# An attention loop with its PSUM banks re-dealt: scores and turned scores as one block per step, turning back by single transposes, projections on other steps

## The chip, the cores and the metric

The kernel runs on one core of a Trainium2 chip. The metric is the device time of the run in microseconds (us). TensorE (PE in the profile) multiplies matrices and writes to PSUM, which has eight banks; VectorE (DVE), ScalarE (ACT) and GpSimd (POOL) do the rest, SyncE (SP) issues DMAs. Each engine works through its own instructions in order, and waits on semaphores for the others.

## The reference

The input is x, 32 sequences of 125 frames with 23 features. Five neighbouring frames form a patch, so a sequence has L = 121 tokens, and there are 3,872 tokens of D = 128 channels:

```python
y = relu(patches @ W.T + b)                       # 115 -> 128
h = (y - mean(y)) * rsqrt(var(y) + eps) * gamma + beta     # over all tokens
a = layernorm(h)
q, k, v = (a @ w.T + b for w, b in ...)           # 8 heads of 16
scores = q @ k.T / 4 + col_bias                   # per sequence and head, 121 x 121
h = h + (softmax(scores) @ v) @ o_w.T + o_b
z = layernorm(h)
e = argmax(z @ Wr + br)                           # one of 8 experts, gate 1
out = h + relu(z @ W1[e] + b1[e]) @ W2[e] + b2[e]
```

col_bias is one number per head and column, from the last valid edge that points at the column. All arithmetic is float32 here.

## The kernel before, in words

A prologue builds the patches, the batch norm's statistics and the weights. Then comes the **attention loop**: 38 steps `t` (`STEPS = B + 6`), one sequence per step, and later pieces of a sequence some steps behind its scores. Two sequences make a pair `p = t // 2`; what is done once for a pair sits in its even or its odd step. After the loop the experts' part goes through 38 tiles of 128 rows.

What a step holds, by the names in the trace (`psS`, `psO`, `psU`, `psB` are PSUM):

- PE `scores` (lines 921, 928): q·k of sequence t and the turned scores k·q of sequence t-1, eight matmuls each (two passes each in the trace), in waves of four that use the four 32-row groups of the array. They come in two halves ("parts") with other matmuls between.
- DVE `nmax` (line 750) takes the maximum of each score row, PE turns it (line 1044), DVE `qm` (line 765) adds it to q, so that the turned scores come out with the maximum subtracted. ACT `PT` (line 495) is exp of the turned scores, PE line 1052 multiplies by V, ACT `OTs` copies, PE line 1005 turns back, DVE `rden` and `on` (736, 738) divide, PE 1025 turns, ACT `oT` copies, PE 1001 multiplies by the output weights, DVE 744 adds to `rows`, DVE 759 squares for the second norm, POOL `rstd2` (365, 370) makes rs2, ACT 489 and DVE `lg` (723) use it.
- Once for a pair, ahead of its scores: ACT `batch_norm` (h0T, 434), PE `transpose_h0` (893), ACT `h0_copy` (h0k, 441), DVE `squares1` (635), POOL `norm1_first` and `norm1_second` (var 345, rs 349, xn 353 and 357, rows 359), PE `transpose_xn` (899), ACT `xT_copy` (448), PE `project` (904) for k and q, DVE `k_copy` (kT, 661), ACT `q_copy` (qT, 453), PE `values` (910), ACT `v_copy` (460).
- For a group of four or two sequences DVE picks experts (`expert_max` and the like), PE ranks rows (`rank_rows`, 967 to 972), DVE gives places (`row_places`), and POOL writes one sequence's rows per step to their places by an indirect DMA (`scatter_rows`, 376).

The order is written out by hand, engine by engine. Three facts of it matter. `h0k` is a single buffer: `h0_copy` of pair p+3 waits (semaphore s_h0b, line 440) until POOL has done `norm1_second` of pair p+2, its last reader. POOL's order in the even step t = 2p is `norm1_first(p + 2)`, one scatter, `rstd2`; in the odd step it is `norm1_second(p + 2)`, one scatter, `rstd2` (lines 388 to 396). And `norm1_first(p + 2)` waits for `squares1(p + 2)`, which DVE does in the even step.

## Time and profile before

| | |
|---|---|
| median of 3 runs | 311.4 us (311.34 to 316.01) |
| the profiled execution | 310.43 us, of which 308.7 us are the span from first to last instruction |
| attention loop at its steady pace | 58.5 to 199.0 us of the span |
| its end, and the experts' bookkeeping | 199.0 to 221.4 us |
| experts' tiles | 221.4 to 308.7 us |
| busy over the span | PE 85%, DVE 61%, ACT 54%, POOL 46% |

The profile's times are in us from the start of the span. A timeline row gives start, duration, engine, line, operation, output<-input, shapes, and in brackets how long the engine had been idle before it and who released it. Close instructions of one kind are merged to one row (x4). [...]

### The profile page before, as it was taken

What the parts mean: (1) busy time and instruction counts of PE and PEld (TensorE: products, weight loads), DVE (VectorE), ACT (ScalarE), POOL (GpSimd) and SP (SyncE); (2) the same over time, 40 slices, a digit from 0 to 9 for tenths busy, and PEclk for the clock granted to TensorE, in tenths of its full rate; (3) what the DMA queues carried; (4) which work ended last, traced back from release to release, by engine and by line L of the source; (5) the groups of instructions that cost most, each with busy time, mean ns of one, the idle gap of its engine ahead of it and who ended that gap; (6) DMA issues with size and microseconds to landing.
All of it is one profiled execution on the core that took longest, in us unless ns stands there. A gap on an engine that the chain in (4) does not pass through costs nothing.

```text
span 308.7 us, 9094 instructions
## 1 busy us (share of the span) xinstructions
PE 263.8 (85%) x2915; PEld 223.6 (72%) x2915; DVE 187.5 (61%) x690; ACT 165.3 (54%) x395; POOL 141.8 (46%) x256
## 2 busy tenths in 40 slices
PE   3898479999999999999999999883099999999960
PEld 2767357778778777877778786562099999999960
DVE  3887233476777768677686777746436556555540
ACT  3861122566655666466664654521067777777730
POOL 7000640343438646476565654347215555555560
PEclk9995575999999999999999999955579999999996
DMA  3200399100001101010010110111243334334200
GB/s 104 71 2 0 98 345 317 47 3 2 2 3 35 32 18 35 19 37 25 28 32 19 34 35 18 35 52 49 74 115 86 101 87 120 98 93 122 79 7 0
DMA packets 15374, 19.14 MB, mean 62 GB/s; under 512 B 4007, under 2 KB 11467, under 8 KB 15328
## 3 DMA queue, kind: packets, MB, share of 16 engines
q1 hardware_dynamic: 11888, 12.15, 14.0%
q0 software_dynamic: 3296, 6.00, 6.6%
q8 instruction: 25, 0.41, 0.6%
q10 hardware_dynamic: 144, 0.41, 0.4%
q14 instruction: 21, 0.17, 0.2%
HBM read 10.58 MB, written 8.47 MB: 62 GB/s over the span
## 4 chain that ended last, share of the span: by engine, by line
PE 71%; issue 9%; POOL 7%; DVE 5%; ACT 3%; DMA 2%; SPq 1%; POOLq 0%; DVEq 0%
PE psS L1089 11%; PE psS L921 10%; PE psB L904 9%; PE psO L1052 5%; PE psO L1100 5%; PE psU L1100 5%; PE psU L1001 4%; PE psU L1005 4%; PE psB L893 3%; POOL region_d L376 3%; PE psB L910 2%; DVE nmax L750 2%; ACT patT L421 2%; PE psU L1044 2%; PE psS L928 2%
## 5 line engine op out<-in xcount | busy, mean ns | idle before, releaser
L404 POOL DMA_INDIRECT out<-y_out,sidx x38 | 36.9, 971 | 45.6 <-DVE y_out L824 41.2
L495 ACT ACTIVATE PT<-psS 121x968 f32<-121x968 f32 x32 | 31.3, 977 | 37.7 <-PE psS L928 37.7
L921 PE MATMUL psS<-kT,qT 32*121 32x121 f32 x512 | 45.7, 294 | 4.9 <-ACT xT L448 2.0
L376 POOL DMA_INDIRECT region_d<-rows,pos x32 | 34.7, 1085 | 31.2 <-DVE pos L709 21.2
L928 PE MATMUL psS<-qm,kT 32*121 32x121 f32 x512 | 45.7, 295 | 0.0
L833 DVE TENSOR_SCALAR hT<-psS,b1T 128x128 f32<-128x128 f32 x76 | 23.3, 347 | 34.9 <-PE psS L1089 34.8
L921 PEld LDWEIGHTS psS<-kT,qT 32*121 32x121 f32 x512 | 34.1, 185 | 13.7 <-issue 9.3
L1089 PE MATMUL psS<-xgT,W_tile 128*128 128x128 f32 x304 | 41.7, 282 | 0.0
L750 DVE TENSOR_REDUCE nmax<-psS 121x8 f32<-121x968 f32 x32 | 37.0, 1157 | 5.6 <-PE psS L921 5.5
L1089 PEld LDWEIGHTS psS<-xgT,W_tile 128*128 128x128 f32 x304 | 38.5, 199 | 0.0
L928 PEld LDWEIGHTS psS<-qm,kT 32*121 32x121 f32 x512 | 33.6, 185 | 0.4 <-DVE qm L765 0.3
L536 ACT ACTIVATE hT<-psS,b1T 128x128 f32<-128x128 f32 x76 | 23.8, 363 | 13.6 <-PE psS L1089 13.3
L510 ACT ACTIVATE W_tile<-W_sb 128x512 f32 x38 | 23.9, 630 | 10.0 <-DVE eid L800 3.7
L765 DVE TENSOR_TENSOR qm<-qT,psU 128x242 f32<-128x242 f32 x32 | 13.0, 407 | 15.8 <-PE psU L1044 15.8
L365 POOL TENSOR_SCALAR var<-ss 121x1 f32<-121x1 f32 x32 | 6.3, 198 | 33.3 <-DVE sq L759 32.8
L736 DVE RECIPROCAL rden<-psU 121x8 f32<-121x8 f32 x32 | 6.7, 208 | 24.4 <-PE psU L1005 24.4
L1052 PE MATMUL psO<-PT,V 121*32 121x121 f32 x512 | 20.3, 276 | 0.4 <-ACT oT L498 0.4
L1100 PE MATMUL psU<-W_sb,hT 128*128 x152 | 20.2, 276 | 0.1
L1100 PE MATMUL psO<-W_sb,hT 128*128 x152 | 20.1, 275 | 0.0
L370 POOL TENSOR_TENSOR rs<-var,minus_half 121x1 f32<-121x1 f32 x32 | 18.0, 564 | 2.7
L904 PE MATMUL psB<-xT,kwT 128*128 128x242 f32 x64 | 19.0, 424 | 0.0
L1100 PEld LDWEIGHTS psU<-W_sb,hT 128*128 128x128 f32 x152 | 18.5, 192 | 0.3 <-issue 0.3
(222 smaller groups left out, 578.4 us busy)
## 6 DMA issues: line engine op xcount, KB each, us to landing
xg<-region_d SPq DMA_DIRECT2D x38, 129.0 KB, 2.1
W_sb<-in_L_ffn_W SPq DMA_DIRECT2D x1, 2048.0 KB, 9.9
region_d<-pads SPq DMA_DIRECT2D x1, 1032.0 KB, 6.9
region_d<-pads SPq DMA_DIRECT2D x1, 903.0 KB, 8.8
out<-y_out,sidx POOLq DMA_INDIRECT x38, 2.8
b_bc<-in_L_ffn_b SPq DMA_DIRECT2D x1, 512.0 KB, 5.1
region_d<-rows,pos POOLq DMA_INDIRECT x32, 3.0
xs<-in_x ACTq DMA_DIRECT2D x1, 402.5 KB, 3.6
```

The costliest lines, as they stand in the source:

```text
L376: pool.indirect_dma_start(region_d, bass.IndirectOffsetOnAxis(pos[0:L, b:b + 1], 0), rows[0:L, b, E:E + ROW], None, bounds_check=E * CAP - ...
L404: pool.indirect_dma_start(out, bass.IndirectOffsetOnAxis(sidx[:, s:s + 1], 0), y_out[:, u, :], None, bounds_check=N - 1, oob_is_err=False) ...
L495: act.activation(PT[0:L, (t - 1) % 2, :, :, :], score_set(t - 1), ACT.Exp).then_inc(s_exp, 1)
L510: act.activation(W1_tile[:, s % 2, :], W1_sb[:, bass.ds(e * F, F)], ACT.Identity).then_inc(f_w1, 1)
L536: ins = act.activation(hT[:, s % 2, c * 128:(c + 1) * 128], psS[:, s % 2, c * 128:(c + 1) * 128], ACT.Relu, bias=b1T[:, bass.ds(e * FC + c ...
L750: dve.tensor_reduce(nmax[0:L, :].rearrange("p (j c) -> p j c", c=HB)[:, :, HD + 1:HD + 3], score_set(t), AX.X, ALU.max, negate=True).then_ ...
L904: return pe.matmul(bank[:, g * PL:(g + 1) * PL], w[:, g * 128:(g + 1) * 128], xT[:, p % 2, :], start=True, stop=True)
L921: ins = pe.matmul(psJ[0:L, t % 2 * HG + j, a * 128:a * 128 + L], qT[rws, t // 2 % 2, a, n0:n0 + L], kT[rws, t // 2 % 2, a, n0:n0 + L], sta ...
L928: ins = pe.matmul(psJ[0:L, u % 2 * HG + j, a * 128:a * 128 + L], kT[rws, u // 2 % 2, a, n0:n0 + L], qm[rws, a, :], start=True, stop=True)
L1052: ins = pe.matmul(psO[j * HB:(j + 1) * HB, a * 128:a * 128 + L], V[0:L, (t - 1) // 2 % 2, (t - 1) % 2, a * HG + j, :], PT[0:L, (t - 1) % 2 ...
L1089: ins = pe.matmul(psS[:, c // 2 * 2 + s % 2, c % 2 * 128:(c % 2 + 1) * 128], W1_tile[:, s % 2, c * 128:(c + 1) * 128], xgT[:, s % 2, :], s ...
L1100: ins = pe.matmul((psU if s % 2 == 0 else psO)[:, 0:D], hT[:, (s + 1) % 2, c * 128:(c + 1) * 128], W2_sb[:, bass.ds(e * F + c * D, D)], st ...
```

## The change

- Scores of sequence t (eight matmuls) and turned scores of t-1 (eight) are one block without halves. Each of psS's four banks belongs to one row group: scores in its first half, turned scores in its second. Before, two banks held sequence t and the other two sequence t-1.
- So DVE's maximum of t waits until the turned scores of t-1 are written too, and ACT's exp of t-1 waits for that maximum (s_max). PE's next block waits for that exp.
- Turning back is two transposes of 128 columns; before, two matmuls with 68 picked columns. `on` becomes two instructions of 64 columns.
- V, h0 and q are in even steps, k in odd ones. Before: k, V and h0 in even steps, q and xn in odd ones. `h0_copy` is at the end of ACT's even step; before it was in the odd one.
- Turning back and everything behind it is one step later; `rstd2` goes along. The norm's POOL parts stay where they are.
- DVE's order: maximum first, then places, lg, qm, k_copy, rden, on, rows, squares of the second norm, `squares1`, and the whole choice of experts at the end of one step.

```diff
@@ -222,7 +222,7 @@
         def ranked(g):
 
             b0, nb = GROUPS[g]
-            return b0 + nb + 4
+            return b0 + nb + 5
...
-        psJ = psS[:, :, :].rearrange("p b (h n) -> p (b h) n", n=256)
-
-        def score_set(t):
-
-            return psJ[0:L, t % 2 * HG:t % 2 * HG + HG, :].rearrange("p j (a n) -> p j a n", a=2)[:, :, :, 0:L]
+        def score_half(turned):
+
+            return psS[0:L, :, turned * 256:turned * 256 + 256].rearrange("p j (a n) -> p j a n", a=2)[:, :, :, 0:L]
...
@@ -392,8 +390,8 @@
                 while done < B and scatter_step(done) <= t and done <= t - 8:
                     scatter_rows(done)
                     done += 1
-                if has(t, 3):
-                    rstd2(t - 3)
+                if has(t, 4):
+                    rstd2(t - 4)
             for b in range(done, B):
                 scatter_rows(b)
...
@@ -475,31 +473,33 @@
 
             for t in range(STEPS):
                 p, even = t // 2, t % 2 == 0
+                if not even and p + 1 < NP:
+                    q_copy(p + 1, psB[:, 0, :])
+                if even and p > 0 and p + 3 < NP:
+                    batch_norm(p + 3)
+                if has(t, 5):
+                    b = t - 5
+                    act.wait_ge(s_r2, b + 1)
+                    act.activation(rows[0:L, b, WX:WX + D], rows[0:L, b, E:E + D], ACT.Identity,
+                                   scale=rs2[0:L, b % 4:b % 4 + 1]).then_inc(s_x2, 1)
+                if has(t, 4):
+                    act.wait_ge(s_OT, t - 3)
+                    act.activation(oT[:, :], psO[:, 256:256 + L], ACT.Identity).then_inc(s_oT, 1)
+                if even and p < NP:
+                    v_copy(p, psB[:, 0, :])
+                if has(t, 1):
+                    act.wait_ge(s_ST, t)
+                    if has(t, 0):
+                        act.wait_ge(s_max, t + 1)
+                    if t >= 3:
+                        act.wait_ge(s_PV, t - 2)
+                    act.activation(PT[0:L, (t - 1) % 2, :, :, :], score_half(1), ACT.Exp).then_inc(s_exp, 1)
                 if has(t, 2):
                     act.wait_ge(s_PV, t - 1)
                     act.activation(OTs[:, :, :], psO[:, 0:256].rearrange("p (a n) -> p a n", a=2)[:, :, 0:L],
                                    ACT.Identity).then_inc(s_OTs, 1)
-                if not even and p + 3 < NP:
+                if even and p + 3 < NP:
                     h0_copy(p + 3, psB[:, 1, :])
-                if even and p > 0 and p + 3 < NP:
-                    batch_norm(p + 3)
-                if has(t, 4):
-                    b = t - 4
-                    act.wait_ge(s_r2, b + 1)
-                    act.activation(rows[0:L, b, WX:WX + D], rows[0:L, b, E:E + D], ACT.Identity,
-                                   scale=rs2[0:L, b % 4:b % 4 + 1]).then_inc(s_x2, 1)
-                if has(t, 1):
-                    act.wait_ge(s_ST, t)
-                    if t >= 3:
-                        act.wait_ge(s_PV, t - 2)
-                    act.activation(PT[0:L, (t - 1) % 2, :, :, :], score_set(t - 1), ACT.Exp).then_inc(s_exp, 1)
-                if has(t, 2):
-                    act.wait_ge(s_OT, t - 1)
-                    act.activation(oT[:, :], psO[:, 256:256 + L], ACT.Identity).then_inc(s_oT, 1)
-                if even and p < NP:
-                    v_copy(p, psB[:, 1, :])
-                if not even and p + 1 < NP:
-                    q_copy(p + 1, psB[:, 0, :])
                 if not even and p + 2 < NP:
                     xT_copy(p + 2, psB[:, 1, :])
 
...
@@ -713,44 +713,42 @@
 
             for t in range(STEPS):
                 p, even = t // 2, t % 2 == 0
-                if not even and p + 1 < NP:
-                    k_copy(p + 1)
-                if even and p >= 1 and p + 2 < NP:
-                    squares1(p + 2)
-                if has(t, 4):
...
+                if has(t, 0):
+                    dve.wait_ge(s_S, t + 1)
+                    if t > 0:
+                        dve.wait_ge(s_ST, t)
+                    dve.tensor_reduce(nmax[0:L, :].rearrange("p (j c) -> p j c", c=HB)[:, :, HD + 1:HD + 3], score_half(0),
+                                      AX.X, ALU.max, negate=True).then_inc(s_max, 1)
+                for g in range(NG):
+                    if ranked(g) == t:
+                        row_places(g)
+                if has(t, 5):
+                    b = t - 5
...
+                if has(t, 0):
+                    dve.wait_ge(s_nT, t + 1)
+                    dve.tensor_tensor(qm[:, :, :], qT[:, p % 2, :, t % 2 * L:t % 2 * L + L],
+                                      psU[:, 0:L].unsqueeze(1).to_broadcast([128, 2, L]), ALU.add).then_inc(s_qm, 1)
+                if not even and p + 1 < NP:
+                    k_copy(p + 1)
+                if has(t, 4):
+                    dve.wait_ge(s_P, t - 3)
                 if has(t, 3):
...
+                if has(t, 4):
+                    b = t - 4
...
                         dve.wait_ge(s_v2, b - 3)
                     dve.scalar_tensor_tensor(out=sq2[0:L, b % 2, :], in0=rows[0:L, b, E:E + D], scalar=1.0, in1=rows[0:L, b, E:E + D],
                                              op0=ALU.mult, op1=ALU.mult, accum_out=ss2[0:L, b % 4:b % 4 + 1]).then_inc(s_sq2, 1)
...
+                if even and p >= 1 and p + 2 < NP:
+                    squares1(p + 2)
+                for g in range(NG):
+                    if ranked(g) - 1 == t:
+                        expert_max(g)
+                        expert_rank(g)
+                        expert_onehot(g)
+                        expert_seen(g)
...
-            def scores(t, part):
-
+            def scores(t):
+
+                p, n0 = t // 2, t % 2 * L
                 for a in range(2):
...
-                            if part == 1 and a == 1 and i == 1:
-                                ins.then_inc(s_ST, 1)
-                if part == 0:
-                    ins.then_inc(s_half, 1)
+                    for j in range(HG):
+                        rws = slice(j * HB, (j + 1) * HB)
+                        ins = pe.matmul(psS[0:L, j, a * 128:a * 128 + L], qT[rws, p % 2, a, n0:n0 + L],
+                                        kT[rws, p % 2, a, n0:n0 + L], start=True, stop=True)
+                ins.then_inc(s_S, 1)
+
+            def scores_T(t):
+
+                p, n0 = t // 2, t % 2 * L
+                for a in range(2):
+                    for j in range(HG):
+                        rws = slice(j * HB, (j + 1) * HB)
+                        ins = pe.matmul(psS[0:L, j, 256 + a * 128:256 + a * 128 + L], kT[rws, p % 2, a, n0:n0 + L],
+                                        qm[rws, a, :], start=True, stop=True)
+                ins.then_inc(s_ST, 1)
...
@@ -980,81 +979,76 @@
             for t in range(STEPS):
                 p, even = t // 2, t % 2 == 0
 
+                if has(t, 2):
+                    pe.wait_ge(s_exp, t - 1)
                 if has(t, 0):
-                    if t >= 2:
-                        pe.wait_ge(s_exp, t - 1)
+                    if t > 0:
+                        pe.wait_ge(s_max, t)
                     if even:
                         pe.wait_ge(s_kT, p + 1)
                         pe.wait_ge(s_qs, 2 * p + 2)
+                    scores(t)
                 if has(t, 1):
                     pe.wait_ge(s_qm, t)
-                if t <= B:
-                    scores(t, 0)
-
...
-                if has(t, 2):
-                    pe.wait_ge(s_OTs, t - 1)
+                    pe.wait_ge(s_OTs, t - 2)
                     for a in range(2):
-                        ins = pe.matmul(psU[0:L, 272 + a * HG * (HD + 1):272 + (a + 1) * HG * (HD + 1)], OTs[:, a, :],
-                                        ident[:, :].rearrange("p (j c) -> p j c", c=HB)[:, :, 0:HD + 1], start=True, stop=True)
+                        ins = pe.transpose(psU[0:L, 258 + a * 113:258 + a * 113 + 128], OTs[:, a, :], ident[:, :])
                     ins.then_inc(s_bT, 1)
...
+                if even and p < NP:
+                    values(p, psB[:, 0, :])
+                if even and p + 3 < NP:
                     if p > 0:
-                        pe.wait_ge(s_qs, 2 * p + 2)
+                        pe.wait_ge(s_xT, p + 2)
+                    transpose_h0(p + 3, psB[:, 1, :])
+                if not even and p + 1 < NP:
+                    pe.wait_ge(s_qs, 2 * p + 4)
                     for g in range(2):
                         ins = project(p + 1, g, psB[:, 0, :], kwT)
                     ins.then_inc(s_k, 1)
...
+                if even and p + 1 < NP:
+                    pe.wait_ge(s_Vs, p + 1)
                     for g in range(2):
                         ins = project(p + 1, g, psB[:, 0, :], qwT)
                     ins.then_inc(s_q, 1)
...
                 if not even and p + 2 < NP:
-                    pe.wait_ge(s_Vs, p + 1)
                     pe.wait_ge(s_h0k, min(p + 4, NP))
+                    for g in range(NG):
+                        if ranked(g) == t:
+                            pe.wait_ge(r_pick, g + 1)
                     transpose_xn(p + 2, psB[:, 1, :])
```

ACT, of the instructions for one pair, from `h0_copy` on. Before (odd step; h0k is the copy of h0, qT that of q, PT is exp):

```order
L441 ACTIVATE h0k<-psB 121x274 [waits s_h0b,s_h0]
L489 ACTIVATE rows<-rows,rs 121x128 [waits s_r2]
L495 ACTIVATE PT<-psS 121x968 [waits s_PV,s_ST]
L498 ACTIVATE oT<-psO 128x121 [waits s_OT]
L453 ACTIVATE qT<-psB,qk_col 128x242 [waits s_q]
L453 ACTIVATE qT<-psB,qk_col 128x242
L448 ACTIVATE xT<-psB 128x242 [waits s_V,s_xn_T]
```

The change (end of an even step, start of the odd one):

```order
L496 ACTIVATE PT<-psS 121x968 [waits s_PV,s_max,s_ST]
L499 ACTIVATE OTs<-psO 128x242 [waits s_PV]
L439 ACTIVATE h0k<-psB 121x274 [waits s_h0b,s_h0]
L451 ACTIVATE qT<-psB,qk_col 128x242 [waits s_q]
L451 ACTIVATE qT<-psB,qk_col 128x242
L483 ACTIVATE rows<-rows,rs 121x128 [waits s_r2]
L487 ACTIVATE oT<-psO 128x121 [waits s_OT]
```

h0k's copy is now behind OTs of the even step and directly ahead of the two copies of q; before, q's copies came after exp and oT, and three instructions lay between.

DVE, of an even step with no experts in it, before, from qm (q plus turned maximum) on:

```order
L765 TENSOR_TENSOR qm<-qT,psU 128x242 [waits s_nT,s_ST]
L635 SCALAR_TENSOR_TENSOR sq,ss<-h0k 121x128 [waits s_sq1,s_v1,s_h0k]
L635 SCALAR_TENSOR_TENSOR sq,ss<-h0k 121x128
L723 SCALAR_TENSOR_TENSOR lg<-rows,rs,br_bc 121x8 [waits s_r2]
L736 RECIPROCAL rden<-psU 121x8 [waits s_bT]
L738 TENSOR_TENSOR on<-psU,rden 121x128 [waits s_rd]
L744 TENSOR_TENSOR rows<-psU,rows 121x137 [waits s_h0b,s_P]
L750 TENSOR_REDUCE nmax<-psS 121x4x2 [waits s_S]
```

The change, an even step and the first row of the odd one:

```order
L720 TENSOR_REDUCE nmax<-psS 121x4x2 [waits s_ST,s_S]
L728 SCALAR_TENSOR_TENSOR lg<-rows,rs,br_bc 121x8 [waits s_r2]
L732 TENSOR_TENSOR qm<-qT,psU 128x242 [waits s_nT]
L741 RECIPROCAL rden<-psU 121x8 [waits s_bT,s_P]
L744 TENSOR_TENSOR on<-psU,rden 121x64 [waits s_rd]
L744 TENSOR_TENSOR on<-psU,rden 121x64
L751 TENSOR_TENSOR rows<-psU,rows 121x137 [waits s_h0b]
L757 SCALAR_TENSOR_TENSOR sq,ss<-rows 121x128 [waits s_v2,s_sq2,s_h1]
L635 SCALAR_TENSOR_TENSOR sq,ss<-h0k 121x128 [waits s_sq1,s_v1,s_h0k]
L635 SCALAR_TENSOR_TENSOR sq,ss<-h0k 121x128
L720 TENSOR_REDUCE nmax<-psS 121x4x2 [waits s_ST,s_S]
```

The two squares of h0k stood right behind qm; now they are the last thing of the even step.

PE, the odd step of the change, up to the turning of the maximum:

```order
L920 MATMUL psS<-kT,qT 121x121 [waits s_max,s_exp]
L920 MATMUL psS<-kT,qT 121x121 x7
L930 MATMUL psS<-qm,kT 121x121 [waits s_qm]
L930 MATMUL psS<-qm,kT 121x121 x7
L999 MATMUL psO<-ident,on 128x121 [waits s_OTs,s_on]
L1005 MATMUL psU<-ident,OTs 121x128 [waits s_OTs,s_h1]
L1005 MATMUL psU<-ident,OTs 121x128
L904 MATMUL psB<-xT,kwT 128x242 [waits s_xT,s_qs]
L904 MATMUL psB<-xT,kwT 128x242 [waits s_xT]
L1020 MATMUL psU<-owX,oT 121x137 [waits s_oT]
L1030 MATMUL psU<-ident,nmax 128x121 [waits s_max]
```

k's projection, the output matmul (L1020) and the turning of the maximum stand one behind the other; the first waits for q's copies (s_qs). Before, in the even step, k's projection was followed by values and the maximum, and the output matmul stood ahead, between the halves of the scores.

## Rows read from the trace of the kernel before

**Rows 1.** The page, part 1: busy us, share of the span, instructions.
```profile
PE 263.8 (85%) x2915; PEld 223.6 (72%) x2915; DVE 187.5 (61%) x690; ACT 165.3 (54%) x395; POOL 141.8 (46%) x256
```

**Rows 2.** Busy us by stretch: loop, its end, experts' tiles.
```profile
58.50:199.00 140.50, 134.93 (x1904) 107.58 (x1902) 100.87 (x357) 83.88 (x195) 74.76 (x139) 1.00 0.08 23
199.00:221.40 22.40, 10.68 (x80) 8.05 (x80) 12.25 (x63) 4.37 (x11) 12.62 (x17) 0.54 0.19 51
221.40:308.70 87.30, 74.54 (x646) 73.90 (x646) 43.52 (x190) 53.54 (x151) 36.91 (x38) 0.93 0.30 83
```

**Rows 3.** Line 1044, the turned maximum, steps 2 to 31.
```profile
L1044 PE MATMUL psU<-ident,nmax x30: 268/322/325, 58.5 to 199.0; 121*128 121x121 f32 x30
```

**Rows 4.** Timeline, PE, one even step (122.63 to 128.15).
```profile
121.21 0.37 PE L899 MATMUL psB<-ident,xn 121*128 121x121 f32 x2
...
122.63 0.33 PE L921 MATMUL psS<-kT,qT 32*121 32x121 f32 x1 [0.19 <-ACT qT L453]
...
123.26 0.50 PE L1001 MATMUL psU<-owX,oT 128*121 128x137 f32 x2
...
123.59 0.54 PE L1005 MATMUL psU<-ident,OTs 128*121 128x68 f32 x4
...
124.69 1.08 PE L904 MATMUL psB<-xT,kwT 128*128 128x242 f32 x4
...
125.61 0.27 PE L1025 MATMUL psO<-ident,on 121*128 121x121 f32 x1
...
126.22 0.68 PE L910 MATMUL psB<-vwT,xT 128*121 128x128 f32 x4
...
126.74 0.27 PE L1044 MATMUL psU<-ident,nmax 121*128 121x121 f32 x1
...
127.49 0.73 PE L893 MATMUL psB<-idX,h0T 128*121 128x137 f32 x4
...
128.15 0.36 PE L921 MATMUL psS<-kT,qT 32*121 32x121 f32 x1
```

**Rows 5.** Timeline, DVE, the same step.
```profile
122.28 0.28 DVE L635 SCALAR_TENSOR_TENSOR sq<-h0k 121x128 f32<-121x128 f32 x1
...
124.17 0.21 DVE L736 RECIPROCAL rden<-psU 121x8 f32<-121x8 f32 x1 [0.69 <-PE psU L1005]
...
124.62 0.29 DVE L744 TENSOR_TENSOR rows<-psU,rows 121x137 f32<-121x137 f32 x1
124.83 1.16 DVE L750 TENSOR_REDUCE nmax<-psS 121x8 f32<-121x968 f32 x1
...
127.58 0.66 DVE L661 TENSOR_TENSOR kT<-psB,addK 128x484 f32<-128x484 f32 x1
```

**Rows 6.** Timeline, POOL, the same step and the start of the next.
```profile
122.88 0.21 POOL L345 TENSOR_SCALAR var<-ss 121x2 f32<-121x2 f32 x1 [0.26 <-DVE sq L635]
...
125.00 1.10 POOL L376 DMA_INDIRECT region_d<-rows,pos  x1 [0.52 <-issue]
126.28 0.19 POOL L365 TENSOR_SCALAR var<-ss 121x1 f32<-121x1 f32 x1 [0.18 <-DVE sq L759]
...
127.46 0.76 POOL L359 TENSOR_TENSOR rows<-h0k,ob_bc 121x274 f32<-121x274 f32 x1
```

**Rows 7.** Timeline, ACT, the same steps.
```profile
121.57 0.81 ACT L453 ACTIVATE qT<-psB,qk_col 128x242 f32<-128x242 f32 x2
...
124.85 0.98 ACT L495 ACTIVATE PT<-psS 121x968 f32<-121x968 f32 x1 [1.18 <-PE psS L928]
...
128.31 0.40 ACT L441 ACTIVATE h0k<-psB 121x274 f32<-121x274 f32 x1 [0.31 <-PE psB L893]
```

**Rows 8.** Timeline, PE, the loop's first step, with the clock at 0.50.
```profile
45.21 1.98 PE L904 MATMUL psB<-xT,kwT 128*128 128x242 f32 x4
```

**Rows 9.** Busy us by stretch, as rows 2: the experts' tiles begin.
```profile
226.00:228.00 2.00, 2.00 (x11) 2.00 (x11) 0.94 (x4) 0.93 (x3) 0.00 (x0) 0.50 0.44 121
228.00:230.00 2.00, 2.00 (x20) 2.00 (x19) 1.14 (x5) 1.71 (x6) 0.00 (x0) 0.97 0.47 126
```

More of the change, by code:

```diff
@@ L740, in _ @@
-                if has(t, 3):
-                    b = t - 3
-                    dve.wait_ge(s_P, b + 1)
-                    dve.wait_ge(s_h0b, b // 2 + 1)
-                    dve.tensor_tensor(rows[0:L, b, 0:WX], psU[0:L, 128:128 + WX], rows[0:L, b, 0:WX], ALU.add).then_inc(s_h1, 1)
-                for g in range(NG):
-                    if ranked(g) + 1 == t:
-                        row_places(g)
-                if has(t, 0):
-                    dve.wait_ge(s_S, t + 1)
-                    dve.tensor_reduce(nmax[0:L, :].rearrange("p (j c) -> p j c", c=HB)[:, :, HD + 1:HD + 3], score_set(t),
-                                      AX.X, ALU.max, negate=True).then_inc(s_max, 1)
@@ L1017, in _ @@
                     ins.then_inc(s_k, 1)
-                if not even and p + 1 < NP:
-                    pe.wait_ge(s_kT, p + 2)
+                if has(t, 4):
+                    pe.wait_ge(s_oT, t - 3)
+                    pe.matmul(psU[0:L, 121:121 + WX], oT[:, :], owX[:, :], start=True, stop=True).then_inc(s_P, 1)
+                for g in range(NG):
+                    if ranked(g) == t:
+                        pe.wait_ge(s_h0k, min(p + 4, NP))
+                        if g > 0:
+                            pe.wait_ge(r_pick, g)
+                        rank_rows(g)
+                if has(t, 0):
+                    pe.wait_ge(s_max, t + 1)
+                    pe.transpose(psU[:, 0:L], nmax[0:L, :], ident[0:L, 0:L]).then_inc(s_nT, 1)
+                if has(t, 2):
+                    pe.wait_ge(s_exp, t - 1)
+                    pe.wait_ge(s_Vs, (t - 2) // 2 + 1)
+                    if has(t, 4):
+                        pe.wait_ge(s_oT, t - 3)
+                    for a in range(2):
+                        for j in range(HG):
+                            ins = pe.matmul(psO[j * HB:(j + 1) * HB, a * 128:a * 128 + L], V[0:L, (t - 2) // 2 % 2, t % 2, a * HG + j, :],
+                                            PT[0:L, t % 2, j, a, :], start=True, stop=True)
+                    ins.then_inc(s_PV, 1)
+                if even and p + 1 < NP:
+                    pe.wait_ge(s_Vs, p + 1)
                     for g in range(2):
```

106 lines of the change are left out of this document (24 added, 82 removed).

## The prediction, on record before the run

> **What bounds the kernel now.** I read the page first: PE is busy for 85% of the span, no other engine for more than 61% [rows 1]. The stretches then say where: in the attention loop PE is busy 134.93 of 140.50 us at full clock (1.00), in the loop's end only 10.68 of 22.40 us, at a mean clock of 0.54, and in the experts' tiles 74.54 of 87.30 us [rows 2]. The change touches the loop and its end. The turned maximum comes once a step, from 58.5 to 199.0 us in 29 steps [rows 3], so a step takes 4.845 us and a pair 9.69 us. In the timeline of one even step PE goes from one thing to the next with a gap of 0.19 us at most [rows 4]: PE's own work is the pace. The other engines have slack, and the order by hand decides whether it lasts.
>
> **What the change gives PE.** One half of a score block lasts 0.63 us, from 122.63 to the output matmul at 123.26 [rows 4]. Two halves joined save one filling and emptying of the array: not below 0.9 us, not above 1.26 us; I take 1.03, which takes two thirds of the first wave's 0.33 us off. That is 0.23 us per step. Turning back by two matmuls lasts 0.54 us, two transposes of this size last 0.37 us [rows 4], 0.17 us less. Together 0.4 us per step, 12.8 us in 32 steps, if PE stays the pace. Moving k, V, h0 and q between steps adds and removes nothing. On DVE one more instruction of `on` adds some 0.2 us per step (between nothing and the 0.29 us of the row of like size [rows 5]). Running exp behind the maximum adds a chain, from block to block: 1.03 + 1.16 (maximum) + 0.98 (exp) [rows 5, 7] and about 0.4 of handovers, 3.6 us. That is under 4.845, so by itself it is covered.
>
> [...]
>
> **What it breaks.** In ACT's new order the copy of h0 for pair p+3 ends the even step 2p, and q's copies for pair p+1 stand directly behind it. The copy of h0 waits for POOL's `norm1_second(p + 2)`. POOL does that in its step 2p+1, behind `norm1_first(p + 2)`, a scatter and `rstd2`, and `norm1_first` waits for `squares1(p + 2)`, which DVE now does at the very end of step 2p. So ACT stands still from early in the pair until nearly a whole chain of DVE and POOL is done; k's projection waits for q's copies, and on PE the output matmul, the turned maximum, and thus qm and k's copy, queue behind it. The next even step's scores wait for k's copy. This is one closed chain per pair, with nothing parallel:
>
> - Even step, PE to the turned maximum: block 1.03, three transposes 0.45 (the pair's 0.37 plus one more), values 0.52 (126.22 to 126.74), h0 0.66 (127.49 to 128.15), output matmul 0.33 (123.26 to 123.59) [rows 4]: 2.99 us. The output matmul's operand is late by about 0.3, since ACT first waits for rs2 of the odd step.
> - Turned maximum to the next DVE instruction behind qm, 126.74 to 127.58: 0.84 [rows 4, 5]. Then rden, on, rows, 124.17 to 124.91: 0.74, plus 0.2 for the second `on`, 0.3 for the second norm's square, and 0.60 for the two squares of h0k until POOL starts (122.28 to 122.88) [rows 5, 6]. So far 5.97 us.
> - POOL: first norm part and scatter 122.88 to 126.10, 3.22; `rstd2` and second part 126.28 to 128.22, 1.94 [rows 6]. With a gap, 5.2 us.
> - ACT: 0.09 to the start of the h0k copy, 0.40 for it, 0.81 for q's two copies, and 0.25 until PE starts (122.38 to 122.63) [rows 4, 7]: 1.5 us.
> - Odd step: k's projection 0.92 (124.69 to 125.61), output matmul 0.33, maximum turned until k's copy starts 0.84, k's copy 0.66, handover 0.06, and in every other pair the ranking, 0.61 at most (125.61 to 126.22), so 0.3 [rows 4, 5]: 3.1 us.
>
> The sum is 15.8 us per pair in place of 9.69. For pairs without a scatter in the even step (steps before 10) the scatter's 0.52 + 1.10 [rows 6] and the ranking go: 13.9 us. The waiting copy exists for p = 1 to 12, since p = 0 is served by the prologue and there is no h0 of p = 16. So 4 x 13.9 + 8 x 15.8 - 12 x 9.69 = 65.7 us more. Pair 13 has squares but no copy: there the second norm's scale on ACT waits for POOL, about 13.2 us, 3.5 more. Pairs 0, 14 and 15 gain about 1 us in all (0.4 per step, less what waits eat). The loop's end has one more step of turning back and output behind each other, about 2 us more at half clock. At full clock that is 310.4 + 65.7 + 3.5 - 1 + 2 = 380.6 us. The experts' choice at the end of DVE's even step (seven instructions, under 2 us) delays the odd step's maximum to about 9 us after the pair's start; it is needed only at about 13.5, where PE turns it. Its cover is this very stall; without the stall it would cost (third rival).
>
> **The clock.** PE would have nothing to do from about 6.5 us into the pair (0.4 us of transposes after the odd block) until k's projection at 12.6 us. In the trace, where PE is busy 10.68 of 22.40 us the granted clock is 0.54 [rows 2], and in the experts' part it is still 0.50 while PE is fully busy at 226 to 228 us and only then rises to 0.97 [rows 9]. So I expect a fall in each pause and a rise some way into the work behind it. At half clock k's projection lasted 1.98 us instead of 1.08 [rows 4, 8], a factor of 1.83. PE's terms in the chain are 3.3 us in the even and 1.57 us in the odd step. All at half clock: 0.83 x 4.87 = 4.0, less the 0.3 that the late operand then no longer costs, 3.7 us per pair. That is the upper end. The lower is nothing. The odd terms come right behind the pause, the even ones some 4 us later: I take 1.9 us per pair, the odd terms (1.3) and a fifth of the even ones. 12 x 1.9 = 22.8, so 403 us.
>
> **Rivals.**
> - Clock at full all through the loop: 380.6, say 381 us. For it: the loop before holds 1.00 with short pauses. Against: the pause is 6 us.
> - Clock at half nearly all through: 12 x 3.7 = 44.4, and pairs 0, 13, 14 and 15 some 10 more, 435 us. For it: it was slow to return at 226 us.
> - POOL stretched. In the even step's end DVE's choice of experts runs beside `norm1_first`. The nearest rows, POOL's instructions beside DVE's squares and expert work from 122.88 on, show no such stretch [rows 5, 6]. If POOL had to wait for it, 1.5 us in six pairs, 412 us. [...]
> - Only rs2 waits: ACT gets over the copy of h0 early, and the odd step is held only by the second norm's scale, behind POOL's scatter and `rstd2`. Then a pair is 5.97 + 3.22 + 1.03 for POOL, 0.9 for ACT, and 2.2 to 2.5 behind it, 13.2 us with a scatter, 11.3 without: about 348 us. It needs the wait on s_h0b to be met early, and the order rows speak against it.
> - PE stays the pace: if neither wait ends last, a pair is 9.69 - 0.8 and the kernel ends at 298 us, faster. The point from which it decides is 8.9 us: DVE, POOL and ACT would have to bring q's copies within 5 us of the pair's start, against 12.6 in my sum.
> - Experts' choice: without the stall, 1.5 to 1.8 us of DVE ahead of the odd step's maximum in every other pair would eat most of the 12.8 us, about 310 us, no change.
>
> **How the numbers follow.** Chances: the forecast 0.57, full clock 0.14, half clock 0.16, POOL stretched 0.03, only rs2 0.04, PE stays the pace 0.04, experts eat the gain 0.02. The predicted time is 403 us; it is made against the profiled run's 310.4 us, 1 us under the median of 311.4, which is within what I can resolve. The range takes in both clock cases with some room for the sizes (0.5 us per pair is 6 us): 373 to 438 us; the last three cases and misjudged sizes are what it leaves out. Measured against no change, 2% is 6 us, about what a measurement can tell. Slower by over 2%: 0.93; within: 0.03; faster: 0.04.
>
> **What would show it.** In the profile after: ACT idle ahead of the h0k copy (line 439), released by POOL rows, for about 6 to 7 us in each of 12 pairs; PE idle ahead of k's projection, released by ACT qT; loop pairs of 14 to 20 us, those from step 10 on longer by some 1.6; maximum and exp one after the other; the clock going between 0.5 and 1.0; PE busy in the loop not much above half. Right or wrong in parts: three transposes near 0.45 us and the joined block near 1.03 us at full clock. Wrong altogether if ACT's wait at h0k is short, or if a pair ends with PE fully busy.

## The result: 385.3 us, slower by 24%

The changed kernel took 385.3 us (median of 4 runs, 384.6 to 388.4), the kernel before 313.7 us beside it. The ratio is 1.236, 95% interval 1.225 to 1.247. I had forecast 403 us, range 373 to 438.

The page's part 1 of the changed kernel, and its row of the granted clock over 40 slices:

```profile
PE 275.7 (72%) x2851; PEld 229.0 (60%) x2851; DVE 189.8 (50%) x722; ACT 163.8 (43%) x395; POOL 141.5 (37%) x256
...
PEclk9985799899688776958776695889555699999995
```

PE is busy for 11.9 us more than in [rows 1], and the span is 74.2 us longer, so PE mostly stands idle for longer. Where it does is told by the stretches, first of the changed kernel (step 2 to step 30, the end of the loop, the experts' tiles), then of the kernel before for steps 2 to 30. Such a row gives busy us of PE, PEld (weight loads), DVE, ACT and POOL with instruction counts, then the clock granted to TensorE as a share of full speed (1.00), the DMA share and GB/s:

```profile
53.41:262.87 209.46, 148.63 (x1783) 115.73 (x1784) 97.12 (x361) 79.97 (x188) 72.75 (x138) 0.80 0.05 14
267.11:298.44 31.33, 12.78 (x101) 8.73 (x101) 15.54 (x81) 6.81 (x18) 14.40 (x20) 0.53 0.20 54
298.44:382.90 84.46, 74.38 (x645) 74.00 (x644) 43.61 (x190) 52.98 (x150) 36.91 (x38) 0.92 0.30 82
```
```profile
58.48:194.35 135.87, 131.62 (x1848) 105.17 (x1846) 97.53 (x343) 81.72 (x190) 72.92 (x136) 1.00 0.08 22
```

The same 28 steps take 209.5 in place of 135.9 us: 73.6 of the 74.2 us by which the span grew. PE is busy for 71% of them instead of 97%, and its granted clock is 0.80 on average instead of 1.00. The waits of the changed kernel in steps 2 to 30 (total us, times, longest us):

```profile
ACT h0k L439 <- POOL rows L357: 67.4, 12, 6.6
...
PE psB L904 <- ACT qT L451: 56.1, 12, 5.7
...
DVE qm L732 <- PE psU L1030: 39.8, 22, 4.6
...
ACT rows L483 <- POOL rs L368: 15.0, 14, 3.6
```

ACT waits at the copy of h0 in 12 pairs for 67.4 us, and PE at k's projection in 12 pairs for 56.1 us. One pair of the timeline, from its even step's block of scores to k's projection, engine after engine (PE; DVE's second square of h0k; POOL; ACT; PE again):

```profile
186.60 0.79 PE L920 MATMUL psS<-kT,qT 32*121 32x121 f32 x16
187.22 0.59 PE L930 MATMUL psS<-qm,kT 32*121 32x121 f32 x16
187.75 0.33 PE L999 MATMUL psO<-ident,on 121*128 121x121 f32 x1
...
188.13 0.60 PE L910 MATMUL psB<-vwT,xT 128*121 128x128 f32 x4
...
189.27 0.27 PE L1030 MATMUL psU<-ident,nmax 121*128 121x121 f32 x1
...
191.16 0.29 DVE L635 SCALAR_TENSOR_TENSOR sq<-h0k 121x128 f32<-121x128 f32 x1
...
191.55 0.19 POOL L343 TENSOR_SCALAR var<-ss 121x2 f32<-121x2 f32 x1 [3.44 <-DVE sq L635]
...
193.65 1.10 POOL L374 DMA_INDIRECT region_d<-rows,pos  x1 [0.51 <-issue]
...
195.99 0.75 POOL L357 TENSOR_TENSOR rows<-h0k,ob_bc 121x274 f32<-121x274 f32 x1
196.84 0.40 ACT L439 ACTIVATE h0k<-psB 121x274 f32<-121x274 f32 x1 [6.31 <-POOL rows L357]
...
197.13 0.81 ACT L451 ACTIVATE qT<-psB,qk_col 128x242 f32<-128x242 f32 x2
...
197.99 0.77 PE L904 MATMUL psB<-xT,kwT 128*128 128x242 f32 x1 [5.36 <-ACT qT L451]
```

This is the closed chain of the prediction, link by link. How long a pair takes is read from the starts of the turned maximum in even steps (us, pairs p = 1 to 14). Below, "early pairs" are p = 1 to 4 and "late pairs" p = 5 to 12, those with a scatter in both steps and a copy that waits:

| kernel | pairs 1 to 14 | sum of steps 2 to 30 |
|---|---|---|
| before | 9.4 9.5 10.0 9.6 10.0 9.6 10.0 9.6 10.1 9.6 10.0 9.6 9.6 9.0 | 135.9 |
| changed | 10.2 13.5 13.4 15.5 15.4 18.1 15.6 18.3 15.8 18.3 15.7 17.6 12.6 9.4 | 209.5 |

### The profile page after: what moved, and what is told of

The parts are those of the page before. It is cut to its first block, busy times and chain, and to the rows that moved or that the text cites. A ratio compares the mean times of both kernels' runs of the same rounds, so it can differ in the third digit from the quotient of the medians.

```text
span 382.9 us, 9019 instructions
## 1 busy us (share of the span) xinstructions
PE 275.7 (72%) x2851; PEld 229.0 (60%) x2851; DVE 189.8 (50%) x722; ACT 163.8 (43%) x395; POOL 141.5 (37%) x256
## 4 chain that ended last, share of the span: by engine, by line
PE 42%; POOL 20%; issue 19%; DVE 8%; ACT 5%; DMA 2%; POOLq 1%; SPq 1%; DVEq 0%; ACTq 0%
PE psB L904 7%; PE psS L1083 6%; POOL region_d L374 6%; POOL out L402 4%; PE psS L920 3%; PE psO L1094 3%; PE psO L1038 3%; ACT qT L451 3%; POOL rs L347 3%; PE psU L1094 3%; POOL rows L357 3%; PE psU L1020 2%; PE psS L930 2%; PE psB L910 2%; PE psB L893 2%
## 5 line engine op out<-in xcount | busy, mean ns | idle before, releaser
L904 PE MATMUL psB<-xT,kwT 128*128 128x242 f32 x64 | 26.8, 564 | 56.1 <-ACT qT L451 56.1
L904 PEld LDWEIGHTS psB<-xT,kwT 128*128 128x128 f32 x64 | 16.1, 277 | 60.1 <-ACT qT L451 58.5
L439 ACT ACTIVATE h0k<-psB 121x274 f32<-121x274 f32 x15 | 6.0, 399 | 69.4 <-POOL rows L357 68.1
L536 ACT ACTIVATE hT<-psS,b1T 128x128 f32<-128x128 f32 x76 | 23.7, 363 | 14.1 <-PE psS L1083 14.0
L920 PE MATMUL psS<-kT,qT 32*121 32x121 f32 x512 | 25.7, 321 | 4.5 <-DVE kT L661 2.5
L499 ACT ACTIVATE OTs<-psO 128x242 f32<-128x242 f32 x32 | 11.9, 373 | 38.3 <-PE psO L1038 37.9
L920 PEld LDWEIGHTS psS<-kT,qT 32*121 32x121 f32 x512 | 19.3, 208 | 13.9 <-issue 12.3
L1038 PE MATMUL psO<-PT,V 121*32 121x121 f32 x512 | 25.8, 333 | 0.0
L483 ACT ACTIVATE rows<-rows,rs 121x128 f32<-121x128 f32 x32 | 13.0, 405 | 26.3 <-POOL rs L368 26.2
L1020 PE MATMUL psU<-owX,oT 128*121 128x137 f32 x64 | 18.1, 375 | 7.4 <-ACT oT L487 7.4
L930 PE MATMUL psS<-qm,kT 32*121 32x121 f32 x512 | 21.7, 288 | 0.2 <-ACT PT L496 0.2
## 6 DMA issues: line engine op xcount, KB each, us to landing
region_d<-pads SPq DMA_DIRECT2D x1, 903.0 KB, 10.1
```

What stands on the lines that cost most here:

```text
L536: ins = act.activation(hT[:, s % 2, c * 128:(c + 1) * 128], psS[:, s % 2, c * 128:(c + 1) * 128], ACT.Relu, bias=b1T[:, bass.ds(e * FC + c ...
L904: return pe.matmul(bank[:, g * PL:(g + 1) * PL], w[:, g * 128:(g + 1) * 128], xT[:, p % 2, :], start=True, stop=True)
L920: ins = pe.matmul(psS[0:L, j, a * 128:a * 128 + L], qT[rws, p % 2, a, n0:n0 + L], kT[rws, p % 2, a, n0:n0 + L], start=True, stop=True)
L930: ins = pe.matmul(psS[0:L, j, 256 + a * 128:256 + a * 128 + L], kT[rws, p % 2, a, n0:n0 + L], qm[rws, a, :], start=True, stop=True)
L1020: pe.matmul(psU[0:L, 121:121 + WX], oT[:, :], owX[:, :], start=True, stop=True).then_inc(s_P, 1)
L1038: ins = pe.matmul(psO[j * HB:(j + 1) * HB, a * 128:a * 128 + L], V[0:L, (t - 2) // 2 % 2, t % 2, a * HG + j, :], PT[0:L, t % 2, j, a, :], ...
```

## The experiments

Experiments 1, 2, 3 and 5 have two runs each, the others four to six. In the changed kernel PE pauses and its granted clock is lower (0.80 in steps 2 to 30, against 1.00 before), so the times of experiments 1 to 5 hold what the clock costs beside the waits: from 110 to 210 us it was 0.83, 0.91 and 0.83 in experiments 1 to 3 and 0.81 in experiment 5, where the kernel before has 1.00 [rows 2].

**1. The copy of h0 alone out of the way.** The changed kernel, with the copy back in the odd step, behind oT:

```diff
                     act.activation(oT[:, :], psO[:, 256:256 + L], ACT.Identity).then_inc(s_oT, 1)
+                if not even and p + 3 < NP:
+                    h0_copy(p + 3, psB[:, 1, :])
...
-                if even and p + 3 < NP:
-                    h0_copy(p + 3, psB[:, 1, :])
```

> The changed kernel, but the copy of h0 for pair p+3 stands in the odd step again, behind the copy oT, so that q's copies no longer queue behind it. Theory of two waits (the one behind the prediction): the copy of h0 goes off the path of k's projection, but the second norm's scale, which POOL gives only behind its first-norm part and a scatter, now ends last in the odd step: pairs of 11.3 to 13.2 us, 345 to 358 us in all. Rival (the copy of h0 ahead of q's copies is the whole cause): 298 to 312 us.

Measured 349.6 us. Its waits:

```profile
ACT rows L483 <- POOL rs L368: 63.9, 31, 4.0
...
ACT h0k L439 <- POOL rows L357: 7.8, 12, 1.3
```

The wait at h0k falls from 67.4 to 7.8 us, and the one at the second norm's scale rises from 22.7 us (the same window, 55 to 285 us) to 63.9. The second wait takes the first one's place. The whole time is inside the theory's range, its pairs are not: late pairs take 12.7 to 15.3 us where 11.3 to 13.2 were expected, and pairs 1 to 3 only 8.5 to 9.9.

**2. DVE's squares early.** The changed kernel with `squares1(p + 2)` as the first thing in the even step:

```diff
+                if even and p >= 1 and p + 2 < NP:
+                    squares1(p + 2)
                 if has(t, 0):
                     dve.wait_ge(s_S, t + 1)
...
-                if even and p >= 1 and p + 2 < NP:
-                    squares1(p + 2)
```

> The changed kernel, but DVE squares h0k as the first thing of the even step, before the maximum. POOL's first-norm part and scatter then start some 5 us earlier; the second part still queues behind rstd2, which needs the square of the second norm at about 4.8 us. Theory: the copy of h0 comes at about 7 us into the pair in place of 11, pairs of about 11.4 us, 325 to 340 us in all. Rival (POOL's own work is the long part of the chain, and where DVE's squares stand matters by no more than the 0.5 us they take): 378 us or more.

Measured 331.7 us, 54 us less than the changed kernel for moving two instructions that are busy for 0.6 us. The wait at h0k is 29.8 us (11 times), again from 55 to 285 us. The time is inside the theory's range: the place matters and not their length, and the rival falls.

**3. POOL's order alone.**

```diff
                     norm1_first(p + 2)
-                if t % 2 == 1 and t > 1 and p + 2 < NP:
                     norm1_second(p + 2)
+                if has(t, 4):
+                    rstd2(t - 4)
                 while done < B and scatter_step(done) <= t and done <= t - 8:
                     scatter_rows(done)
                     done += 1
-                if has(t, 4):
-                    rstd2(t - 4)
```

> The changed kernel with POOL's order alone changed: both parts of the first norm in the even step, then the second norm's scale, then the scatter. The squares of h0k stay at the end of DVE's even step. Theory (POOL's scatter and second-norm scale are in the chain): the copy of h0 comes about 8.7 us into the pair, a pair is about 13.2 us with or without a scatter, 350 to 365 us in all. Rival (the late squares are the cause, and POOL's order is hidden behind them): 375 us or more.

Measured 363.5 us, inside the theory's range, with a wait at h0k of 44.6 us in 12 pairs (55 to 285 us). The rival falls: POOL's order is not hidden behind the late squares. Late pairs take 12.6 and 14.6 us by turns, where about 13.2 were expected for all.

**4. Both: early squares and POOL's order.**

> The changed kernel with the squares of h0k first in DVE's even step, and with POOL doing both parts of the first norm in the even step ahead of the second norm's scale, and the scatter last. Theory: nothing waits for POOL any more, PE is the pace again, a pair is about 8.9 us plus what DVE's choice of experts costs in every other pair (up to 0.9 us): 298 to 306 us. Rival (the choice of experts at the end of the even step delays the maximum and eats the gain): 309 to 313 us.

Measured 311.8 us, ratio 0.989 (0.982 to 0.995), above the theory's 298 to 306 us. The number is the rival's, but its reason gives the smaller part: pairs 1 to 4, of which the fourth already has a choice of experts, take 8.5, 8.5, 8.6, 9.3 us, pair 5, whose first norm has no scatter ahead of it yet, 8.6, and those behind it 10.7 and 9.8 by turns. A choice of experts goes with 0.7 to 0.9 us more in every other pair, the scatter ahead of the first norm with 1.2 to 1.4 in each. In one of the pairs with no choice of experts:

```profile
131.75 0.20 POOL L343 TENSOR_SCALAR var<-ss 121x2 f32<-121x2 f32 x1
...
134.55 0.40 ACT L438 ACTIVATE h0k<-psB 121x274 f32<-121x274 f32 x1 [2.00 <-POOL rows L357]
...
135.70 1.08 PE L903 MATMUL psB<-xT,kwT 128*128 128x242 f32 x4 [1.05 <-ACT qT L450]
```

POOL begins the first norm at 131.75, though its squares were there at 129.8, behind the scatter of the odd step (130.62 to 131.71). The copy of h0 and k's projection still wait for it.

**5. The two moves alone in the kernel before.** Squares behind qm at the end of the even step, and the copy of h0 at the end of ACT's even step; all else stays:

```diff
-                if even and p >= 1 and p + 2 < NP:
-                    squares1(p + 2)
...
                                       psU[:, 0:L].unsqueeze(1).to_broadcast([128, 2, L]), ALU.add).then_inc(s_qm, 1)
+                if even and p >= 1 and p + 2 < NP:
+                    squares1(p + 2)
...
-                if not even and p + 3 < NP:
-                    h0_copy(p + 3, psB[:, 1, :])
...
                     q_copy(p + 1, psB[:, 0, :])
+                if even and p + 3 < NP:
+                    h0_copy(p + 3, psB[:, 1, :])
```

> The kernel before, with two moves alone: DVE's squares of h0k at the end of the even step (behind qm), and ACT's copy of h0 at the end of the even step. Score halves, banks, turning back and projections stay. Theory (the closed chain squares, POOL, copy of h0, the rest of ACT's odd step is the cause): ACT stands until about 10.7 us into each pair, OTs, exp and q's copies queue behind it, pairs of about 15 us, 365 to 380 us in all. Rival (the slow-down needs the joined block, exp behind the maximum, or the moved projections): under 330 us.

Measured 396.9 us, more than the 365 to 380 us that I expected and more than the changed kernel itself. Its late pairs take 16.7 to 17.6 us instead of about 15. In this order still more queues behind the copy, the turning back between the score halves included:

```profile
189.34 0.40 ACT L441 ACTIVATE h0k<-psB 121x274 f32<-121x274 f32 x1 [6.02 <-POOL rows L359]
...
190.06 1.08 PE L1005 MATMUL psU<-ident,OTs 128*121 128x68 f32 x4 [4.79 <-ACT OTs L480]
```

So neither the joined block, nor exp behind the maximum, nor the moved projections are needed for the loss. No run does the reverse, the changed kernel with these two moves alone taken back.

**6. One of the two moves.** The kernel before with the copy of h0 at the end of the even step and the squares where they were:

> The kernel before with one move alone: ACT's copy of h0 at the end of the even step. DVE's squares stay early, behind qm, where POOL started on them 0.25 us into the even step, so the second norm part ends about 5.6 us into the pair, when PE has just finished turning h0. Theory (the move of the copy only hurts together with late squares): ratio 0.99 to 1.02. Rival (the copy ahead of q's copies hurts by itself): 1.05 or more.

The four runs took 311.7, 316.2, 317.3 and 317.3 us, those of the kernel before beside them 309.8 to 314.5 (medians 316.7 and 311.1); there is no interval that tells them apart. In the profiles steps 2 to 30 take 141.3 us against 135.9, with 15.2 us of waits at h0k (10 times, longest 2.2), where the kernel before already has 7.7 (8 times, longest 1.5). The ratio of the medians, 1.018, is within the theory's 0.99 to 1.02, at its edge, and under the rival's 1.05: the copy by itself costs little, if anything. Both moves together cost 82 us (396.9 against the 314.7 beside it). The late squares alone were not tried in the kernel before, so their own share there is not shown; experiment 1, the changed kernel with late squares and the copy in the odd step, took 349.6 us.

**7. What is left: POOL's scatters and k's copy.** As 4, with scatters only in even steps while the loop has scores, and on DVE k's copy ahead of qm:

```diff
...
-                while done < B and scatter_step(done) <= t and done <= t - 8:
+                while (t % 2 == 0 or t >= B) and done < B and scatter_step(done) <= t and done <= t - 8:
...
+                if not even and p + 1 < NP:
+                    k_copy(p + 1)
                 if has(t, 0):
                     dve.wait_ge(s_nT, t + 1)
...
-                if not even and p + 1 < NP:
-                    k_copy(p + 1)
```

> The kernel with early squares and POOL's both norm parts first, and now also: POOL's two scatters of a pair both at the end of the even step, and k's copy ahead of qm on DVE. In the run with early squares and the new POOL order, pairs without scatters took 8.5 us and pairs with them 9.8 to 10.7, ACT's copy of h0 waiting 2.0 us for POOL. Theory (what is left is POOL's scatter of the odd step ahead of the first norm, and k's copy behind qm): pairs of 8.6 to 9.2 us, 296 to 304 us in all. Rival (DVE's choice of experts ahead of the odd step's maximum is what is left): 307 to 313 us.

Measured 300.9 us, ratio 0.966 (0.958 to 0.973): faster than both kernels, and inside the theory's range. Pairs take 8.2 and 9.3 us by turns, steps 2 to 30 take 121.6 us. The two edits were not run one by one, so what each gives is not shown. PE goes on without a gap from turning back to k's projection and the output matmul:

```profile
127.84 0.32 PE L998 MATMUL psO<-ident,on 121*128 121x121 f32 x1
128.00 0.38 PE L1004 MATMUL psU<-ident,OTs 128*121 128x128 f32 x2
128.22 0.98 PE L903 MATMUL psB<-xT,kwT 128*128 128x242 f32 x4
129.04 0.40 PE L1019 MATMUL psU<-owX,oT 128*121 128x137 f32 x2
```

**8. Turning back by matmuls again.** As 7, with the two matmuls of 68 columns and one `on` (DVE's part of the edit is left out here):

```diff
...
-                        ins = pe.transpose(psU[0:L, 258 + a * 113:258 + a * 113 + 128], OTs[:, a, :], ident[:, :])
+                        ins = pe.matmul(psU[0:L, 272 + a * HG * (HD + 1):272 + (a + 1) * HG * (HD + 1)], OTs[:, a, :],
+                                        ident[:, :].rearrange("p (j c) -> p j c", c=HB)[:, :, 0:HD + 1], start=True, stop=True)
```

> As h_pool_k, but turning back by two matmuls with 68 picked columns, as in the kernel before, and on in one instruction. Theory (PE is the pace again, each step costs 0.17 us more): 3 to 6 us more than h_pool_k. Rival (neither is on the path, or DVE is the pace and gains from the single instruction): within 1 us of it, or below.

Measured 300.7 us: the same, as the rival has it. In the profiles the loop's steps 2 to 30 are 2.1 us longer (123.7 against 121.6), and one turning back lasts 0.38 us from start to next start against 0.22:

```profile
126.07 0.54 PE L1001 MATMUL psU<-ident,OTs 128*121 128x68 f32 x4
126.45 1.03 PE L900 MATMUL psB<-xT,kwT 128*128 128x242 f32 x4
```

So the single transposes save the 0.17 us per step that I said, but of the 4.5 us for 28 steps only 2.1 arrive in the loop, and the whole time can't show it. The second `on` that they need on DVE went away in the same run, so the 2.1 us is the sum of both.

**9. The clock by itself.** The changed kernel with useless matmuls in PE's pause (the line that defines `warm`, and the one that keeps the transpose ahead from counting `s_OT` itself, are left out here):

```diff
...
+                if warm(t):
+                    for _ in range(WARM):
+                        ins = pe.matmul(psO[:, 0:PL], kwT[:, 0:128], xT[:, p % 2, :], start=True, stop=True)
+                    ins.then_inc(s_OT, 1)
```

> The changed kernel, with 11 matmuls of 242 columns added on PE in the odd steps 5 to 25, behind turning back and ahead of k's projection, where PE stood idle for 5.4 to 5.7 us; their result is not used, and they last about 4.4 us at full clock, so they end before q's copies are there. Theory (the granted clock falls in each pause, and that costs about 2.7 us of the 16.9 us of a late pair): the clock stays at 1.00 through the loop, late pairs take about 14.2 us, 360 to 368 us in all. Rival (the pairs' length is the chain of POOL, DVE and ACT, and the clock is worth 1 us per pair or less): 374 us or more.

Measured 365.3 us, 20.1 us less than the changed kernel for 121 matmuls more. The stretch from 110 to 235 us in the changed kernel, then here, and one pause here:

```profile
110.00:235.00 125.00, 82.39 (x912) 64.72 (x913) 51.05 (x196) 43.76 (x104) 46.51 (x83) 0.75 0.06 17
```
```profile
110.00:235.00 125.00, 109.82 (x1265) 89.88 (x1263) 61.19 (x231) 48.91 (x122) 54.34 (x97) 0.99 0.07 20
```
```profile
181.33 4.66 PE L1015 MATMUL psO<-xT,kwT 128*128 128x242 f32 x22
...
185.71 0.40 ACT L440 ACTIVATE h0k<-psB 121x274 f32<-121x274 f32 x1 [6.32 <-POOL rows L358]
...
186.87 1.08 PE L905 MATMUL psB<-xT,kwT 128*128 128x242 f32 x4 [0.89 <-ACT qT L452]
```

ACT waits at h0k as long as in the changed kernel (67.5 us in 12 pairs against 67.4), only the clock is another. The eight late pairs take 14.1 to 15.0 us, 117.0 us in all against 135.0: the clock is worth 2.2 us in each. The four early pairs take 51.1 us against 52.5, so there it was worth little.

**10. The choice of experts.** As 7, with `expert_seen` at the end of the odd step:

```diff
                         expert_onehot(g)
-                        expert_seen(g)
+                    if ranked(g) == t:
+                        expert_seen(g)
```

> As h_pool_k, with DVE's last two instructions of the choice of experts (the sum over a group, seen) moved from the end of the even step to the end of the next odd one. In h_pool_k pairs without the choice take 8.2 us and pairs with it 9.3. Theory (the choice delays the odd step's maximum, and with it exp and k's scores): 0.2 to 0.4 us less in every other pair, 2 us in all at most, ratio to the kernel before 0.955 to 0.967. Rival (the ranking on PE makes the difference of 1.1 us): the same as h_pool_k, 0.966, or above.

Measured 300.1 us, ratio 0.957 (0.951 to 0.963). The ratio is inside what the theory expected, but the loop is not shorter: pairs of 8.2 and 9.4 us, 121.6 us for steps 2 to 30, as in 7. The theory falls. The trace of experiment 7 shows where the 1.1 to 1.2 us of a pair with a ranking lie, here beside the pair before it, whose turned maxima start at 125.03, 129.28 and 133.21:

```profile
129.27 0.65 DVE L660 TENSOR_TENSOR kT<-psB,addK 128x484 f32<-128x484 f32 x1
...
130.44 0.70 PE L919 MATMUL psS<-kT,qT 32*121 32x121 f32 x16
...
137.46 0.18 PE L965 MATMUL psB<-oh_bf,before 121*121 121x32 bf16 x1
...
137.97 0.30 PE L1029 MATMUL psU<-ident,nmax 121*128 121x121 f32 x1
138.16 0.19 DVE L704 TENSOR_TENSOR picked_row<-psB,oh_bf 121x32 f32<-121x32 f32 x1 [0.59 <-PE psB L970]
...
138.62 0.66 DVE L660 TENSOR_TENSOR kT<-psB,addK 128x484 f32<-128x484 f32 x1
...
139.53 0.70 PE L919 MATMUL psS<-kT,qT 32*121 32x121 f32 x16 [0.35 <-DVE kT L660]
```

The ranking's own matmuls put 0.51 us (137.46 to 137.97) ahead of the odd step's turned maximum. DVE then waits for their result and gives the places ahead of k's copy, which starts 0.65 us behind the turned maximum instead of beside it, and the next block starts 1.56 us behind it in place of 1.16. The last 0.26 us lie between that block and the even step's turned maximum (3.03 us in place of 2.77). This is read from one trace; no run moves the places behind k's copy.

## Why the prediction was right, and where it was off

**The mechanism held.** The copy of h0 ahead of q's copies, with DVE's squares at the step's end and POOL's scatter and scale between: shown by experiment 5, which makes the loss out of these two moves alone, and by 1 to 4, which take links out, one or two at a time, and are shorter each time. The rival "only rs2 waits" was given 348 us; experiment 1 made that case and took 349.6, which is partly luck: its late pairs took 13.8 us on average against the 13.2 said, with the clock below full (0.83 from 110 to 210 us), which that rival had not counted, and its early ones 8.5 to 13.0 against 11.3. The rival "PE stays the pace", a pair of 8.9 us and 298 us, is what experiments 7 and 8 come to (8.8 and 8.9 us per late pair on average, 300.9 and 300.7).

Of the signs named, ACT's wait at h0k, PE's wait for q's copies and the clock's swings came as said. The waits at h0k were 5.6 us on average, a little under the 6 to 7 said, and PE was busy for 71% of steps 2 to 30, not "much above half". The early pairs fell partly under the 14 to 20 us said (10.2 to 15.5).

**The sum, term by term.** The pair above begins at half clock (the rows under "The clock" below), so the term from its block on is taken from experiment 9, at full clock (1.00 from 175.41 to 178.13 us):

| term | forecast | measured |
|---|---|---|
| joined block | 1.03 | 1.06 (191.03 to 192.09) |
| three transposes | 0.45 | 0.38 (187.75 to 188.13) |
| block to turned maximum, with the late operand | 3.3 | 2.72 (experiment 9, 175.41 to 178.13) |
| turned maximum to POOL's start | 2.7 | 2.28 (189.27 to 191.55) |
| POOL | 5.2 | 5.2 (191.55 to 196.74) |
| ACT to k's projection | 1.5 | 1.25 (196.74 to 197.99) |
| k's projection to the next block | 3.1 | 3.12 (experiment 9: 2.69 without a ranking, 3.55 with it) |
| late pair at full clock | 15.8 | 14.6 (experiment 9) |
| clock, per late pair | 1.9 | 2.2 |
| late pair | 17.7 | 16.9 |
| pairs 1 to 4 | 15.8 each | 10.2, 13.5, 13.4, 15.5 |
| loop's end (from 25.8 us) | +2 | +5.5 |
| before step 2 | 0 | -5.1 |

That joining the halves saves a filling and emptying of the array was my estimate, from the first wave's 0.33 us; the traces show 1.06 us in place of twice 0.63, and not what saves it. The mis-sized terms are PE's and DVE's work ahead of POOL, 1.0 us too much per pair, and ACT's, 0.25 us. On PE most of it is h0's turning with the late operand behind it: 0.66 + 0.3 said, 0.52 measured (177.28 to 177.80 in experiment 9). On DVE I added durations where the next instruction starts before the one before has ended (the two `on` together 0.36 us in place of 0.29 + 0.2), and the 0.84 us from turned maximum to k's copy was longer than the 0.63 us until rden starts here. Pair 1 was counted as a full one, though at t = 2 there is no output matmul and no `rstd2` in the chain; its 10.2 us fits that. The early pairs are 10.7 us less than forecast, the eight late ones 6.7 less. The end was 3.5 us dearer than said, at a mean clock of 0.53, with one more round of turning back and output matmul. The steps before step 2 were 5.1 us shorter, which I had not foreseen: 2.1 us of it is pair 0 (8.5 us in place of 10.6), 3.0 an earlier first turned maximum. No experiment asks why, and in runs with much the same start (7 and 8) the first turned maximum came at 48.95 and 44.87 us, so part of it may be chance. So 403 us was too high by 18 us, nearly all of it in the pairs, and the misses at the end and before step 2 partly cancel.

**The clock.** The direction and the place were right. The size, 22.8 us said and 20.1 measured, is near in part by luck: I had put 1.9 us on each of 12 pairs, and it was 2.2 in the late ones and 1.4 in all four early ones together. In two neighbouring pairs of the changed kernel the clock came back at different times:

```profile
184.00:186.00 2.00, 2.00 (x21) 1.22 (x19) 0.86 (x2) 0.00 (x0) 0.00 (x0) 0.50 0.00 0
186.00:188.00 2.00, 2.00 (x40) 1.57 (x37) 1.14 (x8) 1.22 (x3) 0.65 (x2) 0.79 0.00 0
...
204.00:206.00 2.00, 2.00 (x25) 1.79 (x22) 0.88 (x1) 0.67 (x2) 0.57 (x1) 0.50 0.00 0
206.00:208.00 2.00, 2.00 (x19) 1.83 (x21) 0.53 (x3) 1.25 (x2) 0.00 (x0) 0.67 0.00 0
```

Work begins again at 182.47 and at 197.99, so it had 4.4 us to the full clock in the first pair and 9.3 us in the second. That is most of the difference between pairs of 15.4 to 15.8 and of 17.6 to 18.3 us in the table; with the clock held (experiment 9) they are 14.1 to 14.5 and 15.0, and what is left is the ranking.

**DVE beside POOL.** The rival that had POOL stretched by DVE's choice of experts did not happen: in the pair above the choice ran beside POOL's first instructions (191.38 to 192.89), and POOL took 5.19 us; in the next one, without it, 209.86 to 215.06, 5.2 us. DVE and POOL instructions overlapped in time:

```profile
191.82 0.19 DVE L679 TENSOR_TENSOR eq<-eq,rank 121x32 f32<-121x32 f32 x1
191.89 0.70 POOL L347 TENSOR_TENSOR rs<-var,minus_half 121x2 f32<-121x2 f32 x1
```

POOL's rs started 0.34 us behind var and lasted 0.70 us, as in the pair without the choice (209.86 to 210.20). It is one overlap of 0.12 us between small instructions. A longer one stands in the trace of the kernel before:

```profile
69.20 0.80 DVE L723 SCALAR_TENSOR_TENSOR lg<-rows,rs,br_bc 121x8 f32<-121x8 f32 x1
69.20 0.77 POOL L359 TENSOR_TENSOR rows<-h0k,ob_bc 121x274 f32<-121x274 f32 x1
```

Here it is DVE's lg that lasted 0.80 us, where its 32 instances have a median of 0.23; POOL's rows took 0.75 to 0.77 us in all its 16. In these rows POOL is not stretched, as the forecast had it.

## What to carry to other kernels

When a copy into a single buffer is moved earlier on an in-order engine, look up who reads the buffer last, on which engine and behind what, and then what stands behind the copy; a wait that was met by the reader's early place is no longer met when the reader's input moves too. In the kernel before, the copy's move alone cost about 5 us in the loop of one profile (and no difference that the whole times can show), and with two squares of 0.6 us moved as well it cost 82 us, because they closed a chain through four engines. When such a chain is found, sum it once round from start-to-start times of the trace, and add the clock of the engine that is left to idle: 2.2 us per late pair here.

## What the runs showed of the hardware

Useless matmuls in a pause made a kernel 20 us faster (385.3 to 365.3 us) by holding the granted clock at 0.97 (60 to 110 us) and 0.99 (110 to 235 us) in place of 0.86 and 0.75. After pauses of 5.7 and 5.4 us the work that followed kept PE fully busy, and the full clock was back 4.4 us after its start in one pair and 9.3 us in the next.

POOL's chain of norm, scatter and second norm took 5.2 us with DVE's small two-input instructions beside its start (191.55 to 196.74) and without them (209.86 to 215.06). DVE's lg, 0.23 us at the median of 32, lasted 0.80 and 0.79 us where it ran beside the 0.77 us of POOL's rows (kernel before, 69.20 and 78.64 us).
